# Attention and routed experts on one core: heads, head section, turns and last experts in another order

## The reference

```python
q = (layernorm(x) @ Wq + bq)              # (8, 112, 16 heads, 16)
k, v = ctx @ Wk + bk, ctx @ Wv + bv       # (8, 375, 16 heads, 16)
x = x + tanh(g_xattn) * (softmax(q k^T / 4) v @ Wo + bo)
xt = layernorm(x).reshape(896, 256)
probs = softmax(xt @ wg); idx = argmax(probs)
# token t has place n in its expert, kept where n < 112
x = x + tanh(g_ffn) * kept * probs[idx] * (xt @ W[idx]^T + b[idx])
```

## Time and profile before

| | us |
|---|---|
| three runs, median (lowest to highest) | 185.61 (184.95 to 186.53) |
| the profiled execution | 185.55 |
| its span, first to last instruction | 183.8 |
| TensorE busy | 169.8 (92%) |
| VectorE busy | 128.7 (70%) |
| POOL busy | 86.4 (47%) |
| ScalarE busy | 80.7 (44%) |

### The profile page before, as it was taken

How to read it: one execution, slowest core, us unless ns; L and a number is a source line. 1 busy time by engine, 2 the same in 40 slices (tenths; PEclk the granted TensorE clock), 3 DMA queues, 4 the chain that set the end, 5 groups by cost and what they waited for, 6 DMA issues and landing times.

```text
span 183.8 us, 4666 instructions
## 1 busy us (share of the span) xinstructions
PE 169.8 (92%) x1799; PEld 119.6 (65%) x1799; DVE 128.7 (70%) x325; ACT 80.7 (44%) x174; POOL 86.4 (47%) x112
## 2 busy tenths in 40 slices
PE   7999979997899999999999999799689989999992
PEld 2557446674587768868766886666467876468740
DVE  5878787838278859858875988895876547755642
ACT  2114131377546817645671764356357760013100
POOL 7297948346991198563027007631040057304650
PEclk9999999999999999999999999999999999999998
DMA  5995838687375357616737532886050005387220
GB/s 153 303 259 123 187 86 208 164 197 186 92 167 136 128 129 168 211 52 156 208 100 168 162 115 69 194 255 220 0 154 4 0 23 180 117 239 199 65 61 25
DMA packets 26029, 26.04 MB, mean 142 GB/s; under 512 B 9677, under 2 KB 24409, under 8 KB 26008
## 3 DMA queue, kind: packets, MB, share of 16 engines
q1 hardware_dynamic: 24322, 23.04, 48.0%
q0 software_dynamic: 864, 2.07, 3.7%
q10 hardware_dynamic: 822, 0.64, 1.3%
HBM read 8.89 MB, written 5.06 MB: 76 GB/s over the span
## 4 chain that ended last, share of the span: by engine, by line
PE 65%; DVE 13%; SPq 5%; DMA 5%; issue 4%; ACT 4%; POOL 3%; DVEq 0%; ACTq 0%; POOLq 0%
PE pj L500 9%; PE pv L576 8%; PE sT L561 7%; PE pj L517 6%; PE sc L531 6%; PE sT L832 4%; PE sc L832 3%; PE pj L813 3%; DVE nmax L1097 3%; DMA ctx_sb<-in_ctxT 3%; PE pj L509 3%; PE misc L590 3%; SPq L364 2%; DMA x_sb<-in_x 2%; SPq L358 2%
## 5 line engine op out<-in xcount | busy, mean ns | idle before, releaser
L1097 DVE TENSOR_REDUCE nmax<-sc 112x1 f32<-112x375 f32 x112 | 58.4, 539 | 23.6 <-PE sc L531 19.6
L945 ACT ACTIVATE prob<-sT 128x448 f32<-128x448 f32 (+1 forms) x96 | 50.0, 545 | 38.1 <-PE sT L561 37.5
L561 PE MATMUL sT<-q,k 128*128 128x112 bf16 x384 | 31.7, 213 | 2.6 <-ACT prob L945 2.0
L1412 POOL TENSOR_SCALAR ve<-mv 112x1 f32<-112x1 f32 (+2 forms) x12 | 2.9, 238 | 66.2 <-DVE mv L1167 58.9
L531 PE MATMUL sc<-k,q 126*128 126x375 bf16 x104 | 31.7, 325 | 1.5 <-DVE nmax L1097 1.3
L561 PEld LDWEIGHTS sT<-q,k 128*128 128x128 bf16 x384 | 24.3, 98 | 13.2 <-ACT prob L945 4.8
L500 PE MATMUL pj<-ctx_sb,wk_sb 128*128 128x375 f32 x64 | 23.3, 485 | 0.9 <-DVE rest_q L1085 0.6
L576 PE MATMUL pv<-prob,v_sb 128*32 128x112 f32 (+1 forms) x768 | 21.8, 261 | 0.0
L576 PEld LDWEIGHTS pv<-prob,v_sb 128*32 128x32 f32 (+1 forms) x768 | 18.0, 110 | 3.6 <-issue 2.7
L517 PE MATMUL pj<-wv_sb,ctx_sb 128*128 128x256 f32 (+1 forms) x72 | 18.9, 384 | 0.0
L1428 POOL TENSOR_TENSOR parts_k<-rest_k,parts_k 128x750 bf16<-128x750 f32 x8 | 12.5, 1562 | 7.1 <-ACT parts_k L899 7.1
(11 more groups left out here) (178 smaller groups left out, 276.6 us busy)
## 6 DMA issues: line engine op xcount, KB each, us to landing
k<-parts_k SPq DMA_DIRECT2D x48, 187.5 KB, 3.0
q<-parts_q SPq DMA_DIRECT2D x48, 56.0 KB, 2.5
ctx_sb<-in_ctxT SPq DMA_DIRECT2D x8, 281.2 KB, 4.8
wT_sb<-in_wT SPq DMA_DIRECT2D x8, 256.0 KB, 3.0
slots<-xin SPq DMA_DIRECT2D x1, 1799.0 KB, 8.3
xin<-slots SPq DMA_DIRECT2D x8, 112.9 KB, 2.2
xin<-slots SPq DMA_DIRECT2D x8, 112.0 KB, 2.8
out<-rows SPq DMA_DIRECT2D x1, 672.0 KB, 4.3
```

The source lines that it names most:

```text
L561: mm = pe.matmul(st[n % 2][:, j * NQ:(j + 1) * NQ], k6_flat[:, b % RING, from_key:from_key + CK], q6[:, b % RING, h, :], start=True, stop= ...
L945: nc.scalar.activation(prob[0:rows_here, n, :], st[n % 2][0:rows_here, 0:4 * NQ], ACT.Exp, scale=SCALE).then_inc(s_p, 1)
L1097: nc.vector.tensor_reduce(nmax[:, h:h + 1], scores_bank(b, i)[0:NQ, 0:NK], axis=AX.X, op=ALU.max, negate=True).then_inc(s_max, 1)
```

## The change

Four parts. In the turns, heads 0 to 3 of a batch move from its own turn to the end of the turn before, and the other heads, the split and the turning of the maxima come earlier. The late lists follow: batch 6 has 12 heads left, turn_max(6) and the first four heads of batch 7 stand earlier. In the head the order of several steps changes on every engine; the three transfers that lay the high part of batch 0's queries are issued by ScalarE behind leave_hi_q(0), ahead of both values copies, and not by SP. At the end dense(1, 3) becomes two products of one expert each, in two banks.

```diff
--- before.py
+++ after.py
-HEADS = ((0, 1), (2, 3), (4, 5), (6, 7), (), (8, 9), (10,), (11, 12), (), (13, 14, 15), (), ())
+HEADS = ((4, 5), (6, 7), (8,), (9,), (), (10, 11), (12,), (13, 14), (15,), (), (), ())
+NEXT_HEADS = (((),) * 9 + ((0,), (1,), (2, 3)), ((),) * 10 + ((0, 1), (2, 3)))
...
-PV_AT, WO_AT, X2T_AT, LOGITS_AT, MAX_AT = (0, 6), 5, 1, 3, (8, 11)
+PV_AT, WO_AT, X2T_AT, LOGITS_AT, MAX_AT = (0, 6), 5, 1, 3, (8, 9)
...
-REST_AT, TURN_AT, SUMS_AT, SCALE_AT, BACK_AT, ADD_AT, STAT_AT, SPLIT_AT = (5, 5), 1, 1, 2, 3, 7, (9, 11), (6, 9)
+REST_AT, TURN_AT, SUMS_AT, SCALE_AT, BACK_AT, ADD_AT, STAT_AT, SPLIT_AT = (5, 5), 1, 1, 2, 3, 7, (9, 11), (6, 8)
...
 def heads_in(t, n):
-    return (REST_HEADS if t == 1 else HEADS)[n]
+    own = (REST_HEADS if t == 1 else HEADS)[n]
+    return [(t, h) for h in own] + [(t + 1, h) for h in at(NEXT_HEADS, t)[n]]
...
-        warm = v_sb[:, 0, 0, 0:8, :].rearrange("p h d -> p (h d)")
+        warm = prob[:, UNITS - 1, 0:256]
...
-        dense_banks = ((sc[0], sc[1], st[0], st[1]), (st[0], st[1], pv, sc[0]))
+        dense_banks = ((sc[0], sc[1], st[0], st[1]), (st[0], st[1], pv))
+
+        def dense_at(tile, e):
+            if tile == 1 and e >= 6:
+                return sc[e - 6][0:NQ, 0:D]
+            return dense_banks[tile][e // 2][0:NQ, e % 2 * D:(e % 2 + 1) * D]
...
                     lay_keys(b, part)
-                    sp.wait_ge(ready, queries_of(b))
-                    lay_queries(b, part)
+                    if b or part:
+                        sp.wait_ge(ready, queries_of(b))
+                        lay_queries(b, part)
...
             first_keys(0)
+            first_keys(1)
             pe.wait_ge(s_ident, 1)
             turn_xn(0)
-            first_keys(1)
             pe.wait_ge(s_wqh, 16)
             pe.wait_ge(s_xnTe, 1)
             first_queries()
...
             project_q(1, 1)
+            project_k(0, 0)
+            first_scores(2)
+            project_k(0, 1)
+            first_scores(3)
+            project_q(0, 0)
+            project_q(0, 1)
             pe.wait_ge(s_wv, 16)
             project_v(0, 0)
             project_v(0, 1)
-            first_scores(2)
-            project_k(0, 0)
-            first_scores(3)
-            project_k(0, 1)
-            project_q(0, 0)
-            project_q(0, 1)
             pe.wait_ge(s_rest, queries_of(1))
             project_v(0, 2)
...
-                    for h in heads[0:1]:
-                        scores(t, h)
+                    for b, h in heads[0:1]:
+                        scores(b, h)
...
-            late_scores(6, 0, 1)
+            late_scores(6, 4, 5)
             half_of_probs_v(4, 1)
-            late_scores(6, 2, 3)
+            late_scores(6, 6, 7)
...
             project_v(6, 0)
-            late_scores(6, 4, 5)
+            late_scores(6, 8, 9)
...
-            late_scores(6, 6, 7)
+            late_scores(6, 10, 11)
             project_v(6, 1)
             logits(3)
-            late_scores(6, 8, 9)
+            late_scores(6, 12, 13)
             through_wo(4)
             late_units(5, 2)
-            late_scores(6, 10, 11)
+            late_scores(6, 14, 15)
             project_v(6, 2)
             late_units(5, 3)
-            late_scores(6, 12, 13)
+            turn_max(6)
             late_units(5, 4, 5)
-            late_scores(6, 14, 15)
+            late_scores(7, 0, 1)
             half_of_probs_v(5, 0)
+            late_scores(7, 2, 3)
             late_units(5, 6, 7)
-            turn_max(6)
-
-            late_scores(7, 0, 1)
-            late_units(5, 8, 9)
-            late_scores(7, 2, 3)
-            late_units(5, 10, 11)
+
+            late_units(5, 8, 9, 10, 11)
             half_of_probs_v(5, 1)
             late_scores(7, 4, 5)
...
+            def last_dense(e):
+                if e == 6:
+                    pe.wait_ge(s_xinTe, E)
+                at = dense_at(1, e)
+                for c in range(2):
+                    pe.matmul(at, x2T[:, LAST, c, :], wT_sb[:, e, c, :], start=(c == 0), stop=False)
+                pe.matmul(at, pick[:, e, :], be_rows[:, :], start=False, stop=True).then_inc(s_dense, 1)
...
             dense(1, 2)
-            dense(1, 3)
+            last_dense(6)
+            last_dense(7)
...
         def _(act):
+            act.dma_start(wkh_sb, wkh.rearrange("c p n -> p c n")).then_inc(s_wkh, 16)
             act.dma_start(x_sb[:, 0, :], x[0, :, :]).then_inc(s_x, 16)
-            act.dma_start(wkh_sb, wkh.rearrange("c p n -> p c n")).then_inc(s_wkh, 16)
...
+            def lay_first_queries_hi():
+                act.wait_ge(s_qpad, 2)
+                act.wait_ge(s_hi, queries_of(0))
+                for j in range(NPROD):
+                    if Q_PART[j] == 0:
+                        act.dma_start(q6[j:128:APART, 0, :, :], parts_q[:, 0, 0, :, :])\
+                           .then_inc(s_hi_laid[0], 16)
...
             leave_first_keys(0)
+            leave_first_keys(1)
             leave_xnT(0)
-            leave_first_keys(1)
             leave_xnT(1)
...
-            leave_v01(0)
             leave_hi_k(0)
             leave_hi_q(0)
+            lay_first_queries_hi()
+            leave_v01(0)
             leave_v2(0)
...
+            nc.vector.memset(q6_flat[:, 0, :].bitcast(F32), 0.0).then_inc(s_qpad, 1)
             dve.wait_ge(s_row, 1)
...
             statistics(0, 1)
-            nc.vector.memset(q6_flat[:, 0, :].bitcast(F32), 0.0).then_inc(s_qpad, 1)
+            nc.vector.memset(q6_flat[:, 2, :].bitcast(F32), 0.0).then_inc(s_qpad, 1)
             normalise(0, 0, 1)
...
             statistics(1, 3)
-            normalise(1, 1, 3)
             dve.wait_ge(s_qf, 1)
             dve.wait_ge(s_bqc, 16)
-            for n in range(4):
+            first_queries_of(0)
+            normalise(1, 1, 3)
+            for n in range(1, 4):
                 first_queries_of(n)
...
-            late_max(6, 4, 5, 6, 7, 8, 9, 10)
+            late_max(6, 8, 9, 10, 11, 12, 13)
             add_x(4)
-            late_max(6, 11)
+            late_max(6, 14)
             sums_2(4)
-            late_max(6, 12)
+            late_max(6, 15)
             variance_2(4)
-            late_max(6, 13, 14, 15)
             split_max(6)
+            leave_max_rows(6)
             late_max(7, 0)
-            leave_max_rows(6)
...
+            nc.gpsimd.memset(v_sb[:, :, :, :, HD:32], 1.0).then_inc(s_vones, 1)
             first_rstd(0, 0, 1)
...
-            nc.gpsimd.memset(v_sb[:, :, :, :, HD:32], 1.0).then_inc(s_vones, 1)
```

More of the change, by code:

```diff
@@ L713, in _ @@
                             project_v(t, c)
-                    for h in heads[1:]:
-                        scores(t, h)
+                    for b, h in heads[1:]:
+                        scores(b, h)
                     if n == PV_AT[0] and 2 <= t:
@@ L1289, in _ @@
                         rest_of_k(t + 2)
-                    for h in heads[1:]:
-                        take_max(t, h)
+                    for b, h in heads[1:]:
+                        take_max(b, h)
                     if 2 <= t:
```

18 lines of the change are left out of this document (7 added, 11 removed).

## The result

The changed kernel takes 191.26 us (median of four runs, 190.76 to 191.58) against 185.56 in the runs of before beside it: a ratio of 1.030, with a 95% interval from 1.025 to 1.035. It is slower, as forecast, but by 5.7 us in place of 2.8, and outside the range.

A forecast was written before the change was run, and what follows sets the result against it. It took TensorE's issue to bound the turns, with room only in turn 1, late lists and head. Boundaries +2.7, context load -0.5, late lists 0, head +1.1, end -0.5 made +2.8: 188.4 us, range 183.5 to 189.8.

The forecast's parts named there:

- Direction and boundaries: Turn boundaries: scores wait for maxima, 0.57 us each at three, 0.7 into late lists, 0.3 for turn 1 to 2; +2.7.
- Rival B: Turn boundaries: they cost nothing, as a projection's tail or the drain leaves room; 185.7 us, chance 0.17.
- The earlier context load: Turn 5's awaited load: SP starts the next copies some 1.1 us sooner, so the load comes earlier; -0.5 us.
- the 2.0 us are waited away: 0: Late lists: four maxima fewer save VectorE 2.0 us, but TensorE waits for the split, so 0; ends -2.1 and +0.5.
- rival C: Late lists: VectorE paces them, so four maxima moved into turns are worth 2.0 us; 183.6 us, chance 0.20.
- step (a): Head: both key products ahead of batch 0's turned rows; first queries +0.8 us, part returned, +0.4 carried on.
- step (b): Head: batch 0's values products go behind project_q(0), which lands at 23.85 instead of 25.0; 1.15 us gained.
- step (c): Head: three issues hold ScalarE 1.9 us ahead of the last values; project_k(2, 0) at 28.8 instead of 27.67.
- The order of the first two loads: Head: hidden, as TensorE is in its warm-up products until then; 0.
- rival A: Head: the issues don't hold ScalarE; head +0.26, 187.5 us, chance 0.15.
- The end: Last experts: only one of the two last combinations is left behind the last product; -0.5 us, ends -0.6 and -0.3.
- Rival D: Turn boundaries: new heads find their copies not laid and wait 1 us at four boundaries; 192 us, chance 0.03.

The follow-up runs named there:

- spaced: The changed kernel with three score sets instead of four ahead of each turn's boundary, the fourth in the next turn's first unit; 188.65 us, ratio 1.017 to before.
- after_fixed: The changed kernel with SP issuing the copies, old orders of first loads and first keys, and three score sets ahead of each turn's end; 186.81 us, 1.005 to before.
- late1: The changed kernel with batch 6's maxima turned two units later on TensorE; the stretch from 99.92 to 132.56 took 32.64 us, 32.68 in the changed kernel.
- v_late_only: The kernel before with batch 0's keys and queries ahead of its values in the head, SP issuing the copies; 186.50 us, 1.003 to before.
- after_keys: The changed kernel with the second half of the first keys put back behind the first turned rows; keys of batch 2 start at 29.52 us.
- act_lay_only: The kernel before with the three laid copies of batch 0's high queries issued by ScalarE; 190.56 us, 1.020 to before.
- after_sp_lays: The changed kernel with the laid copies of batch 0's high queries issued by SP again; 190.20 us, 1.025 to before.
- head_only: The kernel before with the new head and ScalarE's issues alone; turns, late lists and end as before; 188.65 us, 1.013 to before.
- turn12_only: The kernel before with three of batch 2's score sets taken into turn 1's last units; 185.25 us, 0.997 to before.
- after_x_keys: The changed kernel with batch 0's rows loaded first again and the first keys' second half behind the turned rows; keys of batch 2 start at 29.37 us.
- best3: The kernel before with the new end, earlier context loads and three of batch 2's score sets in turn 1; 184.15 us, 0.991 to before.
- end_only: The kernel before with the last two experts of the last tile in banks of their own alone; 185.61 us, 0.998 to before.
- best2: The kernel before with the new end and each context load from batch 5 on issued a turn earlier; 184.29 us, 0.996 to before.

## Why the prediction was right and wrong

**Direction and boundaries: right in mechanism, short in size.** At the boundary taken as the model (4 to 5) the forecast 1.45 us from head 1 to head 4 measured 1.42, and the waits are those of the score line for the maximum line. Rival B falls with it. Of the other boundaries, 2 to 3 and the one into the late lists came within 0.1 us. Turn 1 to 2 cost 0.61 for 0.3. Only heads 3 and 4 are late there, as forecast, but the price put on them was too small: heads 2 and 3 put unit 11 back by some 0.2 us, and behind that unit (0.19) head 4 waits 0.44 for its bank:

```profile
49.88 0.36 PE L569 MATMUL sT<-q,k 128*128 128x112 bf16 x4
50.51 0.32 PE L539 MATMUL sc<-k,q 126*128 126x375 bf16 x1 [0.27 <-DVE nmax L1118]
```

Turn 3 to 4 cost 0.92 for 0.57: the cast of the maxima took 0.67 us there and 0.17 at the next boundary, beside a GpSimd operation that ends as it does, and the turned maxima waited 0.33 us for VectorE. It took 0.66 to 0.69 in the six other traces with four sets at this boundary, and 0.22 and 0.21 with three, in spaced and after_fixed, where the boundary cost 0.27. The earlier context load was right: turn 4 grew by 0.02, forecast 0.07. Together 2.99, forecast 2.2.

**Late lists: the step "the 2.0 us are waited away: 0" missed +0.5.** It was right that nothing is gained, so rival C falls at its own point: unit 6 of batch 5 starts 13.16 us behind the second half of batch 4 (117.00, 130.16), before 12.64 (111.74, 124.38). The rows tell where the 0.51 arises. From that half to the first transposed units it is 4.78 us for 4.39: the product at 119.69 is 0.40 longer, and the scores wait 0.39 more. From there to unit 6 it is 8.38 for 8.25: the wait for the split, forecast 1.0 and measured 0.8, takes what four scores less would give. And from unit 6 to the second half of batch 5 it is 2.74, as before (2.75), where the forecast had 2.5 (124.6, 127.1): six exponentials of ScalarE pace it, 2.99 us in both traces. Whether a shorter product would give its 0.39 back is not shown: in spaced it took 0.52, but there one set more stands in the stretch, and the lists grew as much. late1 showed that moving the awaited split away uncovers the next bound.

**The head: step (a) failed, step (b) was counted too high, step (c) came out.** Step (a), "carried on, +0.4", cost 0.94: the keys of batch 0 start 11.48 us behind the first keys, and 10.54 in v_late_only, which has the old order of (a). The first queries are 1.02 us late (0.8 forecast), 0.86 of it by the two orders together and 0.16 by a longer warm-up, and nothing of it comes back: from the first queries to the keys of batch 0 it is 7.80 to 7.88 us in every order, 7.80 in v_late_only, and 7.88 also with the normalising put back. The step had counted on 0.4 returned because the first query no longer stood behind the normalising; but rest_k, behind the maxima, sets when the next keys start. The order of the first two loads, put at nothing, counts as much as the keys' order: with it alone the first queries still come 3.47 us behind the first keys, 2.74 before (after_keys).

Step (b) alone gave 1.07 at the copy of the high keys (v_late_only, 1.17 counted from the first keys on); the forecast had 1.55 for it, 1.15 with (a)'s 0.4. The term that was too small is the fourth set of scores. TensorE comes free of it 0.87 us behind the last maxima (22.77), forecast 0.45 (22.2, 22.65), and in the trace of before it is 0.87 as well:

```profile
21.78 0.99 DVE L1118 TENSOR_REDUCE nmax<-sT 112x1 f32<-112x375 f32 x2
23.64 0.70 PE L517 MATMUL pj<-xnT,wq_sb 128*128 128x112 f32 x4
```

Step (c), 4.9 us from there to the keys of batch 2, measured 4.97; the term for issues that hold ScalarE is shown by act_lay_only and after_sp_lays, so rival A falls. But of (c) only 0.91 us are the issues; the rest is the values' place, so that (b) and its part of (c) together never were a gain (+0.36 alone, 0.26 from the first keys on). The runs divide the head without a rest: 0.94 for (a), 0.26 for the values' place, 0.91 for the issues and 0.16 for the longer warm-up, in all 2.27. The sentence of the Trainium skill weighed in the prediction (DMA: Bandwidth & Descriptors, Issuing engines are not separate DMA queues) compares the issue with the transfer, and the trace agrees so far: 0.63 us an issue, 3.7 from issue to landing. The prediction's reading of it, that ScalarE would be held little, does not hold on this path: 1.89 us of held copies in act_lay_only.

**The end: right**, -0.51 for -0.5, though the 1.03 us read as a product with its bias are the product alone: the bias is an instruction of its own in the trace, of 0.27 us at 174.33. The 0.8 us of the routed rows had no term; they vary by execution.

So of 3.23 us between forecast and profiled growth, 1.17 are the head, 0.78 the boundaries, 0.51 the late lists and 0.78 the landing at the end. Rival D, copies that aren't laid in time, is seen nowhere: of the scores' 3.2 us of waits 3.1 are for maxima.

## What to carry to other kernels

Work moved into another stage should be spaced by the pace of the engine that consumes it: four score sets ahead of a boundary cost 0.5 to 0.9 us each time, three cost 0 to 0.45. Count the issues of transfers as work of the engine that issues them, and put none ahead of a copy that TensorE waits for. When a chain of several engines is reordered, look for the next wait before a step is booked as gain: the keys' order, the normalising's place and the later turning, each undone alone, moved 0.13, 0 and 0.04 us.

## What the runs showed of the hardware

The granted clock of TensorE was not expected to matter, with 0.997 and 1.0 in the two profiled executions (before's falls only behind its last combination, from 182.7 us). It does. In head_only TensorE stood partly idle from 44 to 50 us, and the clock fell to 0.50 from 50.1 to 53.5:

```profile
44.00:48.00 4.00, 2.94 (x68) 2.05 (x65) 3.48 (x12) 3.06 (x7) 2.75 (x4) 1.00 0.56 144
48.00:52.00 4.00, 2.99 (x16) 1.89 (x17) 0.81 (x2) 2.67 (x7) 4.00 (x4) 0.76 0.14 37
52.00:56.00 4.00, 4.00 (x60) 2.42 (x59) 1.38 (x3) 0.54 (x1) 4.00 (x3) 0.81 0.86 198
```

Parts of both later stretches run at the lower of the two levels, and batch 4's keys take 1.57 us longer. All eight executions of head_only and act_lay_only have a mean clock below 0.996, and 24 of the 76 of before beside the experiments (187.5 us on average, the others 185.5). With the new turns or with turn12_only it was below that in one execution only, that of after_x_keys, whose clock falls in the head at 30.2, behind 1.39 us of idle TensorE (the same gap left it at 1.00 in the changed kernel). None of the 24 of turn12_only and best3 fell, and 6 of the 29 of before beside them did; of end_only, best2 and v_late_only, which keep the old turns, 8 of 34. The same work in turn12_only, 2.13 us earlier:

```profile
41.87:45.87 4.00, 2.96 (x69) 2.14 (x66) 3.48 (x12) 3.07 (x7) 2.75 (x4) 1.00 0.74 172
45.87:49.87 4.00, 3.46 (x42) 1.99 (x46) 2.37 (x5) 2.67 (x7) 4.00 (x4) 1.00 0.25 73
```

So the sets pulled over the first boundary do pay there: with them the clock stays up. That they do it by filling TensorE's waits for ScalarE is argued from these rows. What decides in an execution of before stays open: in the profiled one TensorE is busy as in head_only in the same stretches (2.93 and 2.99 us of 4), and the clock stays at 1.00.

Three smaller ones. The warm-up products, of which TensorE did nothing else from 1.2 us on, became shorter (0.63 to 0.38 us) at a moment between 4.0 and 7.0 us over the traces, and the first keys started with it, at 6.26 to 7.72: a part of what the executions differ by. The copies that ScalarE issued landed 3.7 us after issue, those of SP in the same stretch 2.3. And some VectorE operations stretch beside some of GpSimd. The product of 0.38 us that takes the heads to their sums' inverse ran 0.81 us before, 1.21 in the changed kernel and 0.52 in spaced, where it began 1.0, 0.6 and 1.3 us after the same GpSimd subtraction of 1.60 us: each time it ended 0.25 behind the subtraction's end. The cast of the maxima, 0.17 us elsewhere, ran 1.31 before beside a GpSimd memset and 0.67 after beside an addition, and ended 0.03 behind either.
